# A linear-attention layer on one core: order of PE's work, accumulators of the last step, and who zeroes V's padding

## The reference, cut to what matters

```python
xn = layernorm(x)                              # x: 4 batches, 512 tokens, width 256
q, k, v = silu(xn @ Wq), silu(xn @ Wk), silu(xn @ Wv)   # 16 heads of 16
# per chunk of 64 tokens and head, with a decay per head:
scores = (q @ k.T) * D ;  o = scores @ v + (q @ S) * q_decay
S      = chunk_decay * S + (k * k_decay).T @ v
o = o * sigmoid((xn @ Wg1) @ Wg2)
o = o * rsqrt(mean(o*o per head) + 1e-5) * norm_w
out = x + (o @ Wo) * silu(fp8(xn) @ fp8(W2))
```

## Time and profile before

| | us |
|---|---|
| median of 3 runs (145.7 to 147.38) | 145.89 |
| the profiled execution | 146.06 |
| its span, first to last instruction | 144.3 |

### The profile page before, as it was taken

One profiled execution on the slowest core, in us unless ns is written; L12 is line 12 of the kernel. 1 busy time (PEld: TensorE's weight loads), 2 busy tenths in 40 slices (PEclk: granted clock), 3 DMA queues, 4 the chain that ended last, 5 costly groups with the idle time before them and its releaser, 6 DMA issues.

```text
span 144.3 us, 7214 instructions
## 1 busy us (share of the span) xinstructions
PE 126.5 (88%) x3134; PEld 107.8 (75%) x3134; DVE 104.3 (72%) x276; ACT 73.7 (51%) x140; POOL 76.3 (53%) x115
## 2 busy tenths in 40 slices
PE   4929999896999999799998999999989999859771
PEld 4829989784987798579875997699768976648650
DVE  0897588999796889477964898489647942944763
ACT  4508678889756675464666266735741663001000
POOL 6972968997928564635573367256507730130030
PEclk9985799999999999999999999999999999986999
DMA  2969300000000002000200001000200020020004
GB/s 79 258 182 365 87 5 0 7 7 2 5 5 5 5 0 77 5 0 5 75 9 0 5 22 60 5 5 15 65 5 5 2 77 5 5 73 5 5 0 145
DMA packets 6847, 6.06 MB, mean 42 GB/s; under 512 B 1376, under 2 KB 6816, under 8 KB 6816
## 3 DMA queue, kind: packets, MB, share of 16 engines
q1 hardware_dynamic: 6816, 5.60, 12.5%
HBM read 3.50 MB, written 2.10 MB: 39 GB/s over the span
## 4 chain that ended last, share of the span: by engine, by line
PE 73%; DVE 14%; issue 6%; POOL 3%; ACT 2%; DVEq 0%; POOLq 0%; ACTq 0%
PE b_o L1091 8%; PE b_q L1135 8%; PE b_q L941 6%; PE b_o L1075 5%; PE b_s L1036 4%; PE b_x L927 3%; PE b_v L954 3%; DVE xn L801 3%; PE b_v L957 3%; PE b_v L955 3%; PE b_q L946 3%; PE b_k L1017 2%; PE b_s L1007 2%; PE b_v L1141 2%; PE b_o L1036 2%
## 5 line engine op out<-in xcount | busy, mean ns | idle before, releaser
L345 POOL TENSOR_TENSOR e_sum<-e_y,e_magic 128x512 f32<-128x512 f32 x8 | 10.4, 1305 | 15.6 <-DVE e_magic L656 15.6
L704 DVE SCALAR_TENSOR_TENSOR og<-gate_tanh,b_o 128x512 f32<-128x512 f32 x8 | 5.5, 686 | 16.0 <-PE b_o L1091 16.0
L1091 PE MATMUL b_o<-probs,v_par 64*32 64x64 f32 x1024 | 15.3, 226 | 0.6 <-issue 0.5
L1135 PE MATMUL b_q<-wo_scaled,on 128*128 128x256 f32 x56 | 14.5, 396 | 1.5 <-DVE on L756 0.8
L355 POOL TENSOR_TENSOR qd<-q_silu,q_decay 128x512 f32<-128x512 f32 x8 | 10.8, 1352 | 8.3 <-ACT q_silu L487 8.3
L383 POOL TENSOR_TENSOR y<-sg,x_sb 128x512 f32<-128x512 f32 x7 | 9.0, 1291 | 11.2 <-DVE sg L777 11.2
L1091 PEld LDWEIGHTS b_o<-probs,v_par 64*32 64x32 f32 x1024 | 10.3, 107 | 5.6 <-issue 4.1
L543 ACT ACTIVATE b_x<-b_x,minus 128x64 f32<-128x64 f32 x8 | 2.3, 285 | 22.4 <-DVE b_x L729 22.4
L365 POOL TENSOR_TENSOR own_mid<-state_mid,head_parity 128x128 f32<-128x128 f32 x8 | 3.2, 400 | 18.7 <-DVE state_mid L684 16.2
L1135 PEld LDWEIGHTS b_q<-wo_scaled,on 128*128 128x128 f32 x56 | 9.9, 189 | 3.8 <-issue 1.3
L671 DVE TENSOR_TENSOR probs<-b_o,decay_mask 128x512 f32<-128x512 f32 x16 | 10.3, 685 | 2.2 <-PE b_o L1036 2.0
(11 more groups left out here) (176 smaller groups left out, 386.8 us busy)
## 6 DMA issues: line engine op xcount, KB each, us to landing
out_dram<-y SPq DMA_DIRECT2D x7, 256.0 KB, 2.1
x_sb<-in_L_attn_x_dram SPq DMA_DIRECT2D x4, 384.0 KB, 5.4
x_sb<-in_L_attn_x_dram SPq DMA_DIRECT2D x2, 256.0 KB, 3.6
w_f<-in_L_attn_Wq_dram SPq DMA_DIRECT2D x1, 256.0 KB, 3.5
w_f<-in_L_attn_Wk_dram SPq DMA_DIRECT2D x1, 256.0 KB, 3.6
w_f<-in_L_attn_Wv_dram SPq DMA_DIRECT2D x1, 256.0 KB, 4.7
w_f<-in_L_ffn_input_dram SPq DMA_DIRECT2D x1, 256.0 KB, 3.8
wo_f<-in_L_attn_Wo_dram SPq DMA_DIRECT2D x1, 256.0 KB, 6.2
```

The source lines that it names most:

```text
L345: g.tensor_tensor(e4_sum[:], e4_y[:, n % 2], e4_magic[:, n % 2], ALU.add).then_inc(s_e4sum, 1)
L1091: mm = t.matmul(ps_o[32 * r:32 * r + 32, c, z:z + C], v_par[rows, u, blk:blk + 2 * E], probs[rows, r, s, i:i + C], start=(half == 0 and s ...
L1135: mm = t.matmul(dst, on[:, kk, s * P:s * P + P], wo_scaled[:, kk], start=(kk == 0 and (s == 0 or n == STEPS - 1)), stop=(kk == KH - 1), sk ...
```

## The change

PE's order in the loop changes by one item: `project_o(n - 1, 0)` stands behind `transpose_k(n + 1)` and ahead of the third quarter of `from_chunk(n)`; `project_o(n - 1, 1)` and `head_sums(n)` stay behind the last quarter. At the start, POOL no longer makes `lag_logdecay` nor zeroes `v_par`: DVE makes the first, ACT writes the second as a copy times 0. ACT casts `wg2`, and DVE forms `wg2_stack` ahead of its work on step 1's exponents. `high_xT(2)`, `low_xT(2)` and `transpose_x(2)` move back by a few places. At the end, o of step 7 is summed in other banks (`b_k` and `b_v`, now one tensor), starting with the state's part while the scores are being masked; `ffn(7)` and its activation move behind `from_chunk(7)`; `root_seed`, `root_step` and `root_cubic` of step 7 run ahead of `head_norm(6)`, and `spread_rs(7)` between the halves of `project_o(6)`; `on` and `sg` have two buffers.

```diff
-        on = sb("on", [P, KH, T])
-        sg = sb("sg", [P, S * D])
+        on = sb("on", [P, 2, KH, T])
+        sg = sb("sg", [P, 2, S * D])
...
+        ps_u_last = b_x[:, 3 * W // 4:W].rearrange("p (k s e) -> p k s e", k=KH, s=S)
+        ps_o_last = b_kv[:].rearrange("p (c z) -> p c z", c=2)[:, :, 0:256]
+        ps_ffn_last = b_o[:, 0:512].rearrange("p (s n) -> p s n", s=S)
...
@@ GpSimd, start @@
-            pool.wait_ge(s_dvec, 2)
-            g.tensor_tensor(lag_logdecay[:], lag_clamped[:].unsqueeze(1).broadcast_to([P, H, C]),
-                            ld_units[:].unsqueeze(2).broadcast_to([P, H, C]), ALU.mult).then_inc(s_laglog, 1)
...
-            for u in range(2):
-                g.memset(v_par[:, u], 0.0).then_inc(s_pool, 1)
...
@@ ScalarE, start @@
             a.activation(table_load[:, 0:1], eps_col[:, 0:1], ACT.Exp)
+            for u in range(2):
+                a.activation(v_par[:, u], eps_col[:, 0:1].broadcast_to([P, 2 * (W + E)]), ACT.Copy, scale=0.0).then_inc(s_vzero, 1)
...
             silu_q(0)
+            act.wait_ge(s_wg2, 64)
+            a.activation(wg2_hi[:], wg2_f32[:], ACT.Copy).then_inc(s_g2w, 1)
...
-            high_xT(2)
             copy_kT(1)
             gate(1)
             find_over(1)
+            high_xT(2)
             scale_y(2)
...
@@ VectorE, start @@
             low_w(0)
+            dve.wait_ge(s_dvec, 2)
+            v.tensor_tensor(lag_logdecay[:], lag_clamped[:].unsqueeze(1).broadcast_to([P, H, C]),
+                            ld_units[:].unsqueeze(2).broadcast_to([P, H, C]), ALU.mult).then_inc(s_laglog, 1)
...
-            low_xT(2)
             put_nan(1)
             gate_o(0)
+            low_xT(2)
...
@@ VectorE, end (n = 7) @@
+            add_state_mid(n)
+            product(n - 2)
             for r in (2, 3, 0, 1):
                 mask(n, r)
-            add_state_mid(n)
-            product(n - 2)
             root_seed(n - 1)
             root_step(n - 1)
             root_cubic(n - 1)
             gate_o(n)
+            root_full(n - 1)
             root_pair(n - 1)
+            root_seed(n)
+            root_step(n)
+            root_cubic(n)
             head_norm(n - 1)
-            rsqrt(n)
+            root_full(n)
+            root_pair(n)
+            head_norm(n)
             product(n - 1)
-            head_norm(n)
...
@@ TensorE, loop @@
                 transpose_k(n + 1)
+                if n == 1:
+                    pe.wait_ge(s_woready, 2)
+                project_o(n - 1, 0)
                 from_chunk(n, 1, 0)
                 from_state(n, 0)
                 from_state(n, 1)
-                ffn(n + 1)
+                if known(n + 2):
+                    ffn(n + 1)
                 from_chunk(n, 1, 1)
-                if n == 1:
-                    pe.wait_ge(s_woready, 2)
-                project_o(n - 1, 0)
                 if known(n + 2):
                     project_o(n - 1, 1)
                     head_sums(n)
...
@@ TensorE, end (n = 7) @@
+            state_steps(n)
+            project_o(n - 2, 1)
             scores(n)
-            project_o(n - 2, 1)
+            from_state(n, 0)
             head_sums(n - 1)
-            state_steps(n)
+            from_state(n, 1)
+            pe.wait_ge(s_sg, n - 1)
+            keep_warm(2, b_q)
             from_chunk(n, 0, 0)
             from_chunk(n, 0, 1)
             from_chunk(n, 1, 0)
-            from_state(n, 0)
-            from_state(n, 1)
             from_chunk(n, 1, 1)
-            keep_warm(5, b_v)
+            ffn(n)
+            keep_warm(2, b_q)
             head_sums(n)
-            keep_warm(2, b_v)
             spread_rs(n - 1)
+            keep_warm(6, b_q)
             project_o(n - 1, 0)
+            spread_rs(n)
             project_o(n - 1, 1)
-            keep_warm(5, b_v)
-            spread_rs(n)
             for s in range(S):
                 project_o(n, s)
```

More of the change, by code:

```diff
@@ L528, in silu_ffn @@
                 need(act, s_sg, n - 2)
-                a.activation(ffn_silu[:, n % 3], b_q[:] if n == 0 else ps_score[0], ACT.Silu, scale=descale[:, 0:1]).then_inc(s_ffn, 1)
+                src = b_q[:] if n == 0 else ps_score[0] if n < STEPS - 1 else b_o[:, 0:512]
+                a.activation(ffn_silu[:, n % 3], src, ACT.Silu, scale=descale[:, 0:1]).then_inc(s_ffn, 1)
             def copy_kT(n):
@@ L626, in _ @@
                 square_o(n)
+            silu_ffn(STEPS - 1)
             square_w(STEPS - 1)
@@ L703, in gate_o @@
                 need(dve, s_on, n - 1)
-                v.scalar_tensor_tensor(out=og[:, n % 2], in0=gate_tanh[:, n % 2], scalar=1.0, in1=ps_o,
+                v.scalar_tensor_tensor(out=og[:, n % 2], in0=gate_tanh[:, n % 2], scalar=1.0, in1=ps_o if n < STEPS - 1 else ps_o_last,
                                        op0=ALU.add, op1=ALU.mult).then_inc(s_og, 1)
@@ L770, in add_x_last @@
                 dve.wait_ge(s_stored[n % 2], 16 * (n // 2))
-                v.tensor_tensor(y[:, n % 2, s], sg[:, s * D:s * D + D], x_sb[:, x_tiles(n).start + NB * s, :], ALU.add).then_inc(s_lasty, 1)
+                v.tensor_tensor(y[:, n % 2, s], sg[:, n % 2, s * D:s * D + D], x_sb[:, x_tiles(n).start + NB * s, :], ALU.add).then_inc(s_lasty, 1)
             def product(n):
@@ L775, in product @@
                 dve.wait_ge(s_ffn, n + 1)
-                need(dve, s_y, n)
-                v.tensor_tensor(sg[:], b_q[:], ffn_silu[:, n % 3], ALU.mult).then_inc(s_sg, 1)
+                need(dve, s_y, n - 1)
+                v.tensor_tensor(sg[:, n % 2], b_q[:] if n < STEPS - 2 else b_o[:, 0:512], ffn_silu[:, n % 3], ALU.mult).then_inc(s_sg, 1)
             def low_w(n):
@@ L806, in _ @@
             low_xT(0)
+            low_w(1)
             stats(1)
-            low_w(1)
             dve.wait_ge(s_actc, 5)
@@ L836, in _ @@
             stats(2)
+            dve.wait_ge(s_g2w, 1)
+            dve.wait_ge(s_pool, 17)
+            v.scalar_tensor_tensor(out=wg2_stack[:], in0=wg2_hi[:].bitcast(F32), scalar=minus_third[:, 0:1], in1=wg2_f32[:],
+                                   op0=ALU.mult, op1=ALU.add).then_inc(s_g2w, 1)
             exponent(1)
@@ L842, in _ @@
             v.tensor_scalar(w2_f32[:], w2_m[:], E4_MIN, E4_MAGIC, ALU.max, ALU.mult).then_inc(s_w2q, 1)
[L844 to L849, removed]
             put_nan(0)
@@ L1061, in from_state @@
                 u = n % 2
+                last = n == STEPS - 1
+                dst = ps_o_last if last else ps_o
                 if c == 0 and pos(n) == 0:
@@ L1074, in from_state @@
                             z = (half * S + s) * C
-                            t.matmul(ps_o[rows, c, z:z + C], st, qd[rows, u, half, s * P + c * C:s * P + c * C + C],
-                                     start=False, stop=False, skip_group_check=True)
+                            t.matmul(dst[rows, c, z:z + C], st, qd[rows, u, half, s * P + c * C:s * P + c * C + C],
+                                     start=(last and half == 0 and s == 0), stop=False, skip_group_check=True)
             def from_chunk(n, half, s):
                 u = n % 2
+                last = n == STEPS - 1
+                dst = ps_o_last if last else ps_o
                 if half == 0 and s == 0:
@@ L1090, in from_chunk @@
                             blk = par * W + (s * HH + half * 4 + r) * 2 * E
-                            mm = t.matmul(ps_o[32 * r:32 * r + 32, c, z:z + C], v_par[rows, u, blk:blk + 2 * E],
+                            mm = t.matmul(dst[32 * r:32 * r + 32, c, z:z + C], v_par[rows, u, blk:blk + 2 * E],
                                           probs[rows, r, s, i:i + C],
-                                          start=(half == 0 and s == 0 and par == 0),
+                                          start=(half == 0 and s == 0 and par == 0 and not last),
                                           stop=(par == 1), skip_group_check=True)
@@ L1131, in project_o @@
                     elif n == STEPS - 2:
-                        pe.wait_ge(s_sg, n)
-                dst = ps_out[:, s] if n < STEPS - 1 else ps_last[s]
+                        pe.wait_ge(s_ffn, STEPS)
+                dst = ps_out[:, s] if n < STEPS - 2 else ps_out_last2[:, s] if n < STEPS - 1 else ps_last[s]
                 for kk in range(KH):
-                    mm = t.matmul(dst, on[:, kk, s * P:s * P + P], wo_scaled[:, kk], start=(kk == 0 and (s == 0 or n == STEPS - 1)),
+                    mm = t.matmul(dst, on[:, n % 2, kk, s * P:s * P + P], wo_scaled[:, kk], start=(kk == 0 and (s == 0 or n == STEPS - 1)),
                                   stop=(kk == KH - 1), skip_group_check=True)
```

50 lines of the change are left out of this document (29 added, 21 removed).

## The result

The changed kernel takes 141.82 us (median of 4; 141.46 to 142.67) against 146.63 for the kernel before in the same measurement: ratio 0.9701, 95% interval 0.9606 to 0.9796. 0.9701 of 146.63 is 142.25, a shade above the upper end of the range (142.2), against a forecast of 139.6. Executions of one kernel fall into a faster and a slower group, and every ratio here compares the faster groups alone, so it need not be the quotient of the medians. The profiled execution took 142.10 (span 140.3) against 146.06.

What follows compares the result with a forecast made beforehand. Limits: start, DVE's xn held by POOL; loop, PE's instruction packets; end, o after the masks. -4.1 + 0.8 + 1.5 - 2.75 - 1.7 = -6.25 from 146.06 gives 139.8, stated as 139.6; range 137.2 to 142.2.

Steps and rivals of the forecast that it cites:

- the masks-to-`gate_o(7)` term: End, from step 7's masks to gate_o(7): about 2.5 us instead of 5.27, -2.75.
- the last term: End, from the start of gate_o(7) to the last y: 10.05 us instead of 11.74, -1.7.
- the stall in `scores(7)`: End, before step 7's masks: an instruction packet boundary falls into the last scores and stalls PE, +1.5.
- the new wait: Loop, before the head sums: PE waits 0.6 us for og_sq in each of steps 1 to 5, +2.9.
- the start: Up to the first head sums: 30.6 instead of 34.67 us, -4.1, bounds -3.0 to -5.3.
- what follows is in series: Start, behind POOL's e_q (5.3 us earlier): ACT's copy through gate_o(0), low_xT(2) and square_o(0) run serially, head sums at 30.6.
- Case (C): Rival: a hole leaves PE's clock low one stretch more, at start or end, +1.7, 141.3 us; chance 0.15.
- The clock row shows 5 in the loop: Sign of being wrong: the profile's clock row at 5 tenths within the loop.
- Case (B): Rival: no stall in scores(7), the packet comes under other work, 137.7 us; chance 0.14.
- (D): Rival: loop's new og_sq wait without relief, packets stall elsewhere there, 2.05 more, 141.7 us; chance 0.08.
- (E): Rival: at the start xn is not held by POOL and takes 3.86 again, 143.7 us; chance 0.07.
- (F): Rival: hole before head_sums drops the clock in each of steps 1 to 6, 149.8 us; chance 0.04.

Runs made afterwards that it cites:

- old_xT: Changed kernel with transpose_x(2), high_xT(2) and low_xT(2) back in their places of before: 139.81 us, ratio 0.9489.
- old_xT_fill_two_q: Changed kernel with step 2's transposes and low_xT(2) in old places, 256-column fillers ahead of ffn(1) and head_sums(0), two q_silu buffers: 137.52 us, ratio 0.9511.
- fill_hole: Changed kernel with three long filler matmuls (512, 512, 256 columns) between ffn(1) and head_sums(0): 138.60 us, ratio 0.9498.
- end_only: Kernel before with the edits of the end alone: 142.41 us, ratio 0.9724.
- loop_only: Kernel before with only project_o(n - 1, 0) moved ahead of the third quarter of from_chunk(n): 146.26 us against 146.74.
- undo_loop: Changed kernel with project_o(n - 1, 0) back behind the last quarter of from_chunk(n): 142.01 us, ratio 0.9736.
- best_undo_loop: Kernel of old_xT_fill_two_q with project_o(n - 1, 0) back behind the last quarter: 137.76 us, ratio 0.9482.
- nine_fillers: Changed kernel with 9 fillers instead of 12 ahead of transpose_x(0), 12 instructions fewer: 142.65 us, ratio 0.9739.
- pool_zeros: Changed kernel with v_par zeroed by POOL again, behind norm_factors(0), not by ACT: 143.56 us, ratio 0.9825.
- start_only: Kernel before with the edits of the start alone: 144.46 us, ratio 0.9872.

## Why the prediction was right or wrong

**Right in direction, in three of the five terms and in the parts of a fourth.** Right were the masks-to-`gate_o(7)` term (-2.75, measured -3.0, with just the 90 matmuls behind the stall that were counted), the last term (-1.7, measured -1.7, 10.05 us), and the stall in `scores(7)` (+1.5 by a count of instructions, measured +1.1). That the last term fits to the hundredth is chance, but the steps on its way agree within 0.25. In the loop, the new wait (0.6 a step, measured 0.38 to 0.47) is paid for by the stalls that go.

**Wrong: the start, -4.1, measured -2.4, outside its bounds of -3.0 to -5.3.** `xn` at 0.3 (0.41) and `q_par` at 10.8 (10.92) were right, and so was what `low_xT(2)` gives back: `old_xT` shows 1.2. Two steps of "what follows is in series" failed. I let POOL's list be last; DVE's was. ACT's `silu_q(1)` waits for POOL's `decay_q(0)` to free the one `q_silu`, 0.68 us that I had not followed; `old_xT_fill_two_q` gives 0.7 back. And I took DVE's durations from the trace of before, where DVE's operation started ahead of POOL's: with POOL shifted, `w_fp` takes 1.69 for 0.76 and the two `head_sum` 1.34 for 0.73. I had used that very effect to explain `xn`, and took it as gone from DVE's list.

**Wrong by more: the clock behind the start.** The sum had nothing for it. Case (C) had one more stretch at the lower level, at the start or at the end, priced at 1.7 and given 0.15; it came as two, at the head of the loop, for 2.1 together (16.55 against 14.41 in `fill_hole`), so the price of one was too high. "The clock row shows 5 in the loop" was a sign of being wrong, and it came. The missing step: I moved PE forward by 5 us and the head sums by 4 or less, and did not ask what PE does in between. The sum itself says that PE's hole there grows; the trace of before had the small ones, 0.3, 0.64 and 0.3, already. Nor was the kernel before free of this loss: `end_only` and `loop_only`, with its start, show it too, so a part of the 2.1 is the luck of the one profiled execution that the sum was set against. With (C) at 2.1 and the start at -2.4 the sum is 146.06 - 6.25 + 1.7 + 2.1 = 143.6; the rest of the loop gave 1.1 more than forecast (-0.3 instead of +0.8), the end 0.65 more: 141.85, measured 142.10.

**The loop without that stretch** is -0.8 over steps 2 to 5: the waits of four steps are more than paid by the stalls that go. ("Stall" is "issue" in the rows.) In `undo_loop` and `best_undo_loop` the move as a whole is worth nothing that can be told in the times.

**The packets.** The Trainium skill's "mostly hidden" ("Runtime: NRT & Kernel Launch", "Instruction fetch mechanics") again disagrees with the trace, which has a stall in `scores(7)` of 0.69, and at another place (0.82) when 12 instructions fewer lie ahead. Case (B) fell. My use of them for gains fell too: what `nine_fillers` won in `scores(7)` was lost at the next stall (0.4 to 1.1) and behind it. (D) did not come, (E) is refuted by `xn`'s 0.41 and by `pool_zeros`, and (F) by every clock row of the loop, all without a low slice behind step 1.

Open: why the same hole brings 3.4 us at the lower clock in `start_only`, `undo_loop` and `nine_fillers`, and 6.8 after and in `pool_zeros`. And how the clock falls out differs from execution to execution: the kernel before has runs from 142.7 to 149.4 in these measurements. Its four with a mean clock of 0.987 or 0.988 took 142.7 to 144.7; the two such executions of the changed kernel took 141.5 and 142.7. So a part of the measured 4.8 seems to be clock that the changed kernel loses less often; the executions are too few, and come from different measurements, to say how much.

## What to carry to other kernels

When one engine is brought forward, ask what it does until the others arrive: a hole in PE's list can be paid twice, the second time in the clock of what follows, and fillers of no use were worth 3 us here. Look for operations of DVE that end with POOL's, as `xn` did: they are held, and it is POOL's work that has to move. And read from the chain of waits whose list passes a delay on: here it was DVE's, while POOL stood idle. Every operation moved across engines changes which of them meet and which of two starts first, and in `w_fp` and `qd` the later one paid. So durations of DVE beside POOL are not to be carried over from the trace of before.

## What was not expected of the hardware

A memset of POOL, which reads nothing, held a DVE operation for its whole length: `xn` 1.94 us beside 1.89 of memsets, 0.41 alone. Two stalls of PE's instructions kept their place in the count of instructions: 12 fewer ahead of them moved one from 3 matmuls ahead of the end of `scores(7)` to 2 behind it, and the next by 6 matmuls.
